# Decoder layer on one core: softmax sums divided out in token space, opening strips issued by three queues, and the shared expert's second layer of three batches moved behind the routed blocks

## The chip, the cores and the metric

The kernel runs on one core of a Trainium2 chip. The core has five engines that run their own instruction streams: PE (TensorE, matmuls and transposes, with its weight loads shown as PEld), DVE (VectorE), ACT (ScalarE), POOL (GpSimd) and SP (SyncE, which here only issues DMAs; POOL and ACT can issue them too). They meet by semaphores. The metric is the time of one execution in device microseconds. The profile is one execution, recorded by the hardware.

## The reference

`x` has 4 batches of 512 tokens with 256 channels. Three layers follow each other, each with a LayerNorm before it and added to `x`: two state-space blocks over the sequence, cross attention to `ctx` (16 heads of 16 channels), and a mixture of experts with a shared expert.

```
x = x + ssm_blocks(layernorm(x))
# attention, on ctx with 512 keys, 16 heads of 16
q = layernorm(x) @ Wq.T + bq;  k = ctx @ Wk.T + bk;  v = ctx @ Wv.T + bv
attn = softmax(q_h @ k_h.T / 4)            # per head, 512 x 512
x = x + concat_h(attn @ v_h) @ Wo.T + bo
# feed-forward
xt = layernorm(x)
probs = softmax(xt @ Wg); the two largest of 8 experts, their weights scaled to sum 1
moe = sum of the two: weight * gelu(xt @ Wu[e]) @ Wd[e]
x = x + moe + gelu(xt @ W1) @ W2           # the shared expert
```

The change touches how the softmax's sums are divided out, how q and k get to their place at the start of attention, and when `gelu(...) @ W2` runs.

## The kernel before, in words

Everything is float32; attention's scores use the same bits as FP32R. The three layers are three phases, with a barrier between them (`phase_border`).

**Attention.** A *unit* `u` is half the heads (eight) of one batch; `NU` = 8 units run one after the other. `project(b)` makes a batch's q and k in six steps on PE: two sets of transposes of the normalised tokens (`xn`), then `k`, `q`, `k`, `q` for 128 channels each; four `v` steps follow. ACT adds the bias and rounds to the high part (`part`, L1001), DVE makes the low part (L1044). `strips` then copies rows of 16 partitions of `part` into `qk`, by small SBUF-to-SBUF DMAs, so that each head's high and low parts stand in one strip of 64 rows. A batch has 64 such DMAs; SP issues 40 and POOL 24 (`n % 8 in (1, 4, 6)`). Batch 0 is copied in two halves, one per unit (32 KB each, semaphores `first_in` and `strips_in`), later batches whole (64 KB each), and only once the last score of the batch two before is done, since `qk` has two places.

Before a unit's scores, DVE must know the largest score of every query row: `pe_max` computes a score tile only for this (L927) and DVE reduces it (L1069). The maxima are transposed to rows (`rows`, L901) and subtracted inside the score matmul (L947). A unit is 16 *slots*. In slot `s`, PE computes score tile `s` (L943, L947), the maximum tile of four slots ahead, which may belong to the next unit (the one after it from slot 12), then one *side* step if `side[(u, s)]` names one, and in odd slots the product with the values (L961). ACT takes the exponential of the score tile (L1008). Score and maximum tiles share three PSUM places of two banks, in a ring (`pair`). Side steps share one single bank (`NONE = 1`): a side step waits until the engine named in `TAKER` has emptied the bank of the one before. The opening runs `project(0)`, the `v` steps of batch 0, the 16 maxima of unit 0 with `project(1)` between the last of them.

The products with the values come out as channels by tokens, four heads in one bank, 32 rows a head, of which row 16 is the softmax sum. ACT copies the bank to `oT` (L1015). A side step `norm` then multiplies with the constant `spread` on PE (L906), which repeats each head's sum over its 32 rows; DVE takes the reciprocal of all 128x512 (L1060), and POOL multiplies `oT` with it (L1172). There are 16 such groups: group 0 of a unit has its `norm` in slot 12, group 1 in slot 1 of the next unit. Group 1 of an odd unit is followed by the output projection of the batch (`out`, L911, slots 3 to 6 of even units), which waits for POOL.

The steps that the slots name: `v` of the next batch in slots 7 to 10 of even units, `project(b + 2)` in slots 3 to 8 of odd units, `rows` in slot 13. The LayerNorm statistics of the next phase and of the batch after next run on DVE and ACT in slots 12 to 15 of even units.

**Feed-forward.** PE makes the shared expert's hidden layer for four batches (L1290), with the routing on DVE beside it, then its second layer (`pe_outputs`, L1300, 32 matmuls a batch; DVE adds them to `xres`, L1530). Then 39 blocks of 128 routed rows run: POOL gathers the rows (L1551), PE transposes, multiplies (L1337), transposes, multiplies (L1352), DVE weighs, POOL scatters to `y_choice` in DRAM (L1557). When all scatters have landed SP loads the results back (L1584), DVE adds two results per token (L1546, `xres` by batch) and SP stores the batches (L1587).

## Time and profile before

| | |
|---|---|
| median of three runs | 1961.38 us (1948.68 to 1962.60) |
| profiled execution | 1958.21 us, its span 1956.6 us |
| busy over the span | PE 87%, DVE 62%, POOL 53%, ACT 43% |
| scan stage (state-space blocks) | 0 to about 1217 us |
| opening of attention | 1219 to 1295 us: PE busy 42.8 us, clock 0.70, DMA share 0.36 |
| units 0 to 7 and the last outputs | 1295 to 1687 us: PE busy 308.9 us, DVE 231.0, ACT 159.7, POOL 47.5, clock 0.87 |
| feed-forward up to the shared second layer | 1687 to 1743 us: PE busy 54.4 us, clock 0.83 |
| shared second layer | 1743 to 1772 us: PE busy 28.8 us, clock 1.00 |
| routed blocks | 1772 to 1932 us: PE busy 159.4 us, clock 1.00 |
| the end | 1932 to 1957 us: PE busy 0.5 us, DVE 10.3, DMA share 0.80 |

The clock is the one that PE was granted, as a share of 2.4 GHz; its two levels are 1.2 and 2.4 GHz. A wait is idle time of an engine, put down to the instruction that ended it; it costs time only if the waiting engine is itself waited for.

### The profile page before, as it was taken

The numbers are of one execution on the slowest core, as the hardware profiler recorded it, in microseconds if no ns is written. First come the engines' busy times: TensorE is split into PE (matmuls) and PEld (weight loads), VectorE is DVE, ScalarE is ACT, GpSimd is POOL, SyncE is SP. The second block draws the span as 40 slices with busy tenths as digits, with TensorE's granted clock in tenths as the row PEclk, the third lists the DMA queues.
The fourth block names the chain that finished last, engine by engine and source line by source line (L and its number), as shares of the span: only waits on it lengthen the run. The fifth ranks groups of instructions, "written<-read, shape, count | busy, mean of one in ns | idle before, by whom it ended". The sixth has DMA issues, their size and how long they took to land.

```text
span 1956.6 us, 27123 instructions
## 1 busy us (share of the span) xinstructions
PE 1705.7 (87%) x10954; PEld 1298.8 (66%) x10954; DVE 1209.4 (62%) x1345; ACT 846.5 (43%) x1188; POOL 1034.0 (53%) x832
## 2 busy tenths in 40 slices
PE   5579899999999999999999998576777889799995
PEld 2468778978978978978879987232332333667763
DVE  3575677777767777766767795465574675233333
ACT  4556546546546446546446442133343346211110
POOL 1557858958948948858859885420200200012441
PEclk9889999999999999999999998688887889799997
DMA  3000000100001001001001210350310400411124
GB/s 140 39 22 34 33 22 23 44 22 29 38 23 40 27 22 45 22 22 45 23 22 77 84 47 13 80 93 32 66 32 6 80 1 1 178 60 36 65 65 158
DMA packets 38123, 93.62 MB, mean 48 GB/s; under 512 B 9137, under 2 KB 21809, under 8 KB 33521
## 3 DMA queue, kind: packets, MB, share of 16 engines
q1 hardware_dynamic: 30416, 75.37, 12.0%
q0 software_dynamic: 7584, 16.53, 3.3%
q8 instruction: 88, 1.44, 0.3%
q14 instruction: 35, 0.28, 0.0%
HBM read 65.52 MB, written 9.57 MB: 38 GB/s over the span
## 4 chain that ended last, share of the span: by engine, by line
PE 63%; POOL 11%; DVE 11%; issue 8%; ACT 3%; SPq 3%; DMA 1%; DVEq 0%; POOLq 0%; ACTq 0%
PE psum L423 18%; POOL hst L688 8%; PE psum L406 7%; PE psum L362 5%; PE psum L1352 3%; PE psum L1337 3%; PE psum L961 3%; PE psum L397 2%; DVE hst L523 2%; DVE uw L448 2%; DVE w_early L1060 2%; PE psum L911 2%; PE psum L943 2%; PE psum L893 2%; POOL filt L666 2%
## 5 line engine op out<-in xcount | busy, mean ns | idle before, releaser
L688 POOL TENSOR_TENSOR hst<-hst,cb 128x512 f32<-128x512 f32 x512 | 662.4, 1314 | 276.6 <-DVE hst L523 275.4
L523 DVE TENSOR_TENSOR_SCAN hst<-dA,psum 128x512 f32<-128x512 f32 x512 | 616.7, 1215 | 294.0 <-PE psum L423 263.1
L423 PEld LDWEIGHTS psum<-filt,c_early 128*128 128x128 f32 x2560 | 316.5, 195 | 56.4 <-issue 29.1
L423 PEld LDWEIGHTS psum<-filt,uT 128*128 128x128 f32 x2560 | 313.7, 194 | 48.4 <-issue 23.4
L423 PE MATMUL psum<-filt,c_early 128*128 128x112 f32 (+1 forms) x2560 | 321.6, 274 | 19.1 <-DVE hst L523 9.5
L423 PE MATMUL psum<-filt,uT 128*128 128x112 f32 (+1 forms) x2560 | 318.9, 272 | 19.2 <-DVE hst L523 9.8
L406 PE MATMUL psum<-ident,hst 128*128 128x128 f32 x2048 | 315.6, 278 | 12.7 <-POOL hst L688 12.0
L406 PEld LDWEIGHTS psum<-ident,hst 128*128 128x128 f32 x2048 | 246.0, 156 | 16.4 <-POOL hst L688 16.0
L626 ACT ACTIVATE dA<-delta,alog 128x512 f32<-128x512 f32 x256 | 181.1, 720 | 133.6 <-DVE hst L523 133.6
L626 ACT ACTIVATE dA<-xres,alog 128x512 f32<-128x512 f32 x256 | 179.5, 719 | 108.0 <-DVE hst L523 107.9
L1008 ACT ACTIVATE pT<-psum 128x1024 f32<-128x1024 f32 x128 | 128.3, 1024 | 197.8 <-PE psum L947 197.2
L1069 DVE TENSOR_REDUCE nmax<-psum 128x2 f32<-128x1024 f32 x128 | 153.5, 1215 | 75.8 <-PE psum L927 75.7
L1172 POOL TENSOR_TENSOR oT<-oT,w_early 128x512 f32<-128x512 f32 x16 | 20.3, 1268 | 330.7 <-DVE w_early L1060 330.7
L362 PE MATMUL psum<-xnT,w_early 128*128 128x512 f32 x256 | 127.4, 627 | 3.1 <-DVE hst L523 1.9
L666 POOL TENSOR_TENSOR filt<-toep,bcol 128x2240 f32<-128x2240 f32 x32 | 129.2, 4038 | 0.0
L448 DVE SCALAR_TENSOR_TENSOR uw<-xraw,w_cv,uw 128x512 f32<-128x512 f32 x96 | 123.3, 1287 | 7.4 <-ACT uw L561 5.2
L1404 ACT ACTIVATE hb<-psum 128x512 f32<-128x512 f32 x39 | 23.3, 598 | 166.5 <-PE psum L1337 166.5
L927 PE MATMUL psum<-qk 64*128 64x512 f32 x256 | 63.2, 497 | 36.4 <-DMA qk<-part 18.0
L1557 POOL DMA_INDIRECT y_choice<-yb,goal x39 | 38.5, 987 | 100.6 <-DVE yb L1521 100.6
L943 PEld LDWEIGHTS psum<-qk 64*128 64x128 f32 x256 | 26.5, 204 | 89.7 <-issue 53.5
L961 PE MATMUL psum<-pT,vt 128*32 128x512 f32 x512 | 76.8, 682 | 7.4 <-ACT pT L1008 7.4
L1551 POOL DMA_INDIRECT xb<-x_hat,origin x39 | 37.9, 972 | 84.0 <-DVE gate_at L1505 72.4
(193 smaller groups left out, 2104.4 us busy)
## 6 DMA issues: line engine op xcount, KB each, us to landing
cb<-c_rows SPq DMA_DIRECT2D x32, 1024.0 KB, 4.7
qk<-part SPq DMA_DIRECT2D x120, 64.0 KB, 2.4
qk<-part POOLq DMA_DIRECT2D x72, 64.0 KB, 4.2
w_up<-up_dram SPq DMA_DIRECT2D x8, 512.0 KB, 7.5
w_down<-down_dram SPq DMA_DIRECT2D x8, 512.0 KB, 14.2
w_up<-y_choice SPq DMA_DIRECT2D x8, 512.0 KB, 8.2
qk<-part SPq DMA_DIRECT2D x80, 32.0 KB, 2.0
xm<-x_dram SPq DMA_DIRECT2D x4, 512.0 KB, 9.0
```

The costliest lines, as they stand in the source:

```text
L362: i = pe.matmul(bk, w_in[:, l, kt, m8 * P:(m8 + 1) * P], xnT[:, kt, :], start=kt == 0, stop=kt == KD - 1)
L406: m = pe.matmul(psum[:, Y0 + et, t * P:(t + 1) * P], hst[:, i % NH, t * P:(t + 1) * P], ident[:], start=n == 0 and t == 0, stop=n == NSTAT ...
L423: m = pe.matmul(bk[:, c * QC:c * QC + CH[c]], uT[k % 2][:, c, et * P:(et + 1) * P], filt[:, f % 2, c, n % GN, 0:CH[c]], start=True, stop=True)
L448: dve.scalar_tensor_tensor(out=dst, in0=xraw[:, j, tap:tap + S], scalar=w_cv[:, l, j, tap:tap + 1], in1=dst, op0=ALU.mult, op1=ALU.add).th ...
L523: dve.tensor_tensor_scan(hst[:, i % NH, :], dA[:, i % NDA, :], bank("v", i), 0.0, ALU.mult, ALU.add).then_inc(scan_done, 1)
L626: act.activation(dA[:, a % NDA, :], delta[k % 2][:, et, :], ACT.Exp, scale=alog[:, k // B, et, n:n + 1]).then_inc(decay_done, 1)
L666: pool.tensor_tensor(filt[:, f % 2], toep[:, :].unsqueeze(1).unsqueeze(1).to_broadcast([P, NCH, GN, QC]), bcol[:, k % 2, :, g * GN:(g + 1) ...
L688: pool.tensor_tensor(h, h, cb[:, q % 2, i // ET % GN, :], ALU.mult).then_inc(g_done, 1)
L943: pe.matmul(o[:, e, :], qk[k0:k0 + KR, b % 2, 1, j, half, kv * P:(kv + 1) * P], qk[k0:k0 + KR, b % 2, 0, j, half, :], start=True, stop=Fal ...
L961: m = pe.matmul(psum[i * HROW:(i + 1) * HROW, PV, :], vt[:, cp, kv, c0:c0 + HROW], pT[:, (m0 + i // 2) % NPT, i % 2, :], start=kv == 0, st ...
L1008: act.activation(pT[:, m % NPT], pair(u, "score", s), ACT.Exp, scale=HDIM ** -0.5).then_inc(pair_act, 1)
L1069: dve.tensor_reduce(nmax[:, u % 2, t, 2 * j:2 * j + 2], pair(u, "max", r), AX.X, ALU.max, negate=True).then_inc(pair_dve, 1)
```

## The change

Four things are changed.

1. *Sums in token space.* `spread`, the 128x512 reciprocal and POOL's product go. A group now takes two side steps. `sums`: PE transposes the four 128x128 tiles of `oT` to tokens by channels; DVE takes the reciprocal of the 16 sums of a row (`rc`) and multiplies the bank by it, each over its head's 32 columns, into `otok`. `norm`: PE transposes `otok` back and ACT copies the bank to `oT`. `out` waits for that copy. POOL has no work but its DMAs.
2. *Order.* `sums` stands in slots 1 and 12, `norm` in 2 and 14, `project(b + 2)` in 3, 4, 5, 7, 9, 11, `out` in 4, 5, 6, 8, `v` in 3, 7, 10, 15. POOL issues its strips of a batch as soon as they may go.
3. *Opening strips.* Batch 0's 64 DMAs a half are issued by SP (24), POOL (24) and ACT (16, ahead of its square root for the second LayerNorm). Later batches stay at 40 and 24.
4. *Shared second layer.* Only batch 0's stays ahead of the routed blocks. That of batches 1 to 3 comes behind the last block, in the four banks which the blocks have left, and DVE's additions of it stand between those of the routed results.

```diff
-            shrink = w_early[:, KD * 2 * P:KD * 2 * P + S]
+            rc = sb(ac, "rc", [P, TB, 4])
+            otok = w_early[:, KD * 2 * P:KD * 2 * P + S]
-            SP_STRIPS, POOL_STRIPS = 40 * 16, 24 * 16
+            OPENING, LATER = (0, 2, 1, 0, 1, 2, 1, 0), (0, 1, 0, 0, 1, 0, 1, 0)
+            FIRST = [16 * UH * OPENING.count(z) for z in range(3)]
+            STRIPS = [16 * UH * LATER.count(z) for z in range(2)]
...
                 if u:
-                    slot(u, 1, u - 1, "norm", 1)
+                    slot(u, 1, u - 1, "sums", 1)
+                    slot(u, 2, u - 1, "norm", 1)
                 if u % 2 == 0:
                     for t in range(TB):
                         if b:
-                            slot(u, 3 + t, b - 1, "out", t)
+                            slot(u, (4, 5, 6, 8)[t], b - 1, "out", t)
                         if b + 1 < B:
-                            slot(u, 7 + t, b + 1, "v", t)
+                            slot(u, (3, 7, 10, 15)[t], b + 1, "v", t)
                 elif b + 2 < B:
-                    for n, name in enumerate(project(b + 2)):
-                        slot(u, 3 + n, *name)
-                slot(u, 12, u, "norm", 0)
+                    for s, name in zip((3, 4, 5, 7, 9, 11), project(b + 2)):
+                        slot(u, s, *name)
+                slot(u, 12, u, "sums", 0)
                 if u + 1 < NU:
                     slot(u, 13, u + 1, "rows", 0)
+                slot(u, 14, u, "norm", 0)
...
+                elif what == "sums":
+                    pe.wait_ge(group_out, group(x, j) + 1)
+                    for t in range(TB):
+                        i = pe.transpose(bk[:, t * P:(t + 1) * P], oT[:, x % 2 * UG + j, t * P:(t + 1) * P], ident[:])
                 elif what == "norm":
-                    pe.wait_ge(group_out, group(x, j) + 1)
-                    i = pe.matmul(bk, spread[:], oT[:, x % 2 * UG + j, :], start=True, stop=True)
+                    pe.wait_ge(*taken(x, "sums", j))
+                    for t in range(TB):
+                        i = pe.transpose(bk[:, t * P:(t + 1) * P], otok[:, t * P:(t + 1) * P], ident[:])
                 elif what == "out":
                     if j == 0:
-                        pe.wait_ge(normed, group(2 * x + 2, 0))
+                        pe.wait_ge(*taken(2 * x + 1, "norm", UG - 1))
...
+                elif what == "norm":
+                    act.wait_ge(*filled_by_pe(x, "norm", j))
+                    act.copy(oT[:, x % 2 * UG + j, :], one(x, "norm", j)).then_inc(taken(x, "norm", j)[0], 1)
...
                     if x == (1, "xn", 0):
+                        strips(act, 2, 0)
                         act_ln_root(LN2[1], TB, 2 * TB)
...
-                elif what == "norm":
-                    dve.wait_ge(*filled_by_pe(x, "norm", j))
-                    dve.reciprocal(shrink, one(x, "norm", j)).then_inc(taken(x, "norm", j)[0], 1)
+                elif what == "sums":
+                    v = one(x, "sums", j).rearrange("p (t i r) -> p t i r", t=TB, r=HROW)
+                    dve.wait_ge(*filled_by_pe(x, "sums", j))
+                    dve.reciprocal(rc[:], v[:, :, :, HDIM]).then_inc(rc_done, 1)
+                    dve.wait_ge(rc_done, group(x, j) + 1)
+                    dve.tensor_tensor(otok.rearrange("p (t i r) -> p t i r", t=TB, r=HROW), v, rc[:].unsqueeze(3).to_broadcast([P, TB, 4, HROW]),
+                                      ALU.mult).then_inc(taken(x, "sums", j)[0], 1)
...
-            def pool_norm(u, g):
-                o = oT[:, u % 2 * UG + g, :]
-                pool.wait_ge(*taken(u, "norm", g))
-                pool.tensor_tensor(o, o, shrink, ALU.mult).then_inc(normed, 1)
...
-                for b in range(B):
+                for b in range(NEAR):
                     pe_outputs(b)
...
+                for b in range(NEAR, B):
+                    pe_outputs_late(b)
...
-                for b in range(B):
-                    r = xres[:, toks(b), :]
-                    dve.wait_ge(y_loaded[b], 16 * TOPK)
-                    for k in range(TOPK):
...
+                for b in range(NEAR, B):
+                    dve_outputs_late(b)
+                    dve_choices(b - 1)
+                dve_choices(B - 1)
```

How the change moves instructions is seen on three engines. First ACT in the opening of attention. Before, behind the four high parts of batch 0 (L1001):

```order
L989 COPY axnT<-psum 128x512 x2
L1001 ACTIVATE part<-psum,b_qk 128x512 x4
L115 ACT_TABLE_LOAD
L115 ACTIVATE stat<-stat,epst 128x4
L989 COPY axnT<-psum 128x512 x2
```

And now:

```order
L1000 COPY axnT<-psum 128x512 x2
L1014 ACTIVATE part<-psum,b_qk 128x512 x4
L1165 DMA qk<-part 16x512 x32
L115 ACT_TABLE_LOAD
L115 ACTIVATE stat<-stat,epst 128x4
L1000 COPY axnT<-psum 128x512 x2
```

Thirty-two DMA issues, sixteen for each half, came between the high parts and the square root (L115), for whose result DVE waits ahead of its first maximum.

Second PE in slots 3 to 6 of unit 3 (an odd unit; L884 or L889 are transposes of `xn`, L893 or L898 the projections). Before:

```order
L893 MATMUL psum<-c_early,w_early 128x512 x2
L961 MATMUL psum<-pT,vt 32x512 x4
L943 MATMUL psum<-qk 128x512 x2
L947 MATMUL psum<-nrow,pick 128x512 x2
L927 MATMUL psum<-qk 128x512 x2
L893 MATMUL psum<-axnT,w_early 128x512 x2
```

And now, from the same `k` step on:

```order
L898 MATMUL psum<-c_early,w_early 128x512 x2
L972 MATMUL psum<-pT,vt 32x512 x4
L954 MATMUL psum<-qk 128x512 x2
L958 MATMUL psum<-nrow,pick 128x512 x2
L938 MATMUL psum<-qk 128x512 x2
L954 MATMUL psum<-qk 128x512 x2
L958 MATMUL psum<-nrow,pick 128x512 x2
L938 MATMUL psum<-qk 128x512 x2
L898 MATMUL psum<-axnT,w_early 128x512 x2
```

Between the `k` and the `q` step there was one slot's score and maximum tile; now there are two slots' worth.

Third DVE behind the last routed block (L1521 or L1550 is the weighing of a block). Before:

```order
L1521 TENSOR_SCALAR yb<-psum,gate_at 128x256
L1513 COPY ht<-psum 128x512
L1521 TENSOR_SCALAR yb<-psum,gate_at 128x256 x2
L1546 TENSOR_TENSOR xres<-xres,w_up 128x1024 x8
```

And now:

```order
L1550 TENSOR_SCALAR yb<-psum,gate_at 128x256 x2
L1565 TENSOR_TENSOR xres<-xres,psum 128x512 x2
L1559 TENSOR_TENSOR xres<-xres,w_up 128x1024 x2
L1565 TENSOR_TENSOR xres<-xres,psum 128x512 x2
L1559 TENSOR_TENSOR xres<-xres,w_up 128x1024 x2
L1565 TENSOR_TENSOR xres<-xres,psum 128x512 x2
L1559 TENSOR_TENSOR xres<-xres,w_up 128x1024 x4
```

The additions of the shared outputs of batches 1, 2 and 3 (L1565) now stand each ahead of the routed results of the batch before (L1559).

## Rows read from the trace of the kernel before

**Rows 1.** Timeline of attention's opening: start us, us, engine line op out<-in [idle before <-releaser].

```profile
1225.70 25.29 SPq L1144 DMA_DIRECT2D qk<-part  x40
1228.34 1.28 ACT L115 ACT_TABLE_LOAD   x1
1237.51 1.42 DVE L124 TENSOR_SCALAR xm<-xres,stat 128x256 f32<-128x256 f32 x4
1251.03 25.24 SPq L1147 DMA_DIRECT2D qk<-part  x40
1253.27 11.40 DVE L1069 TENSOR_REDUCE nmax<-psum 128x2 f32<-128x1024 f32 x10 [14.00 <-PE psum L927]
1265.36 3.78 PE L893 MATMUL psum<-c_early,w_early 128*128 128x512 f32 x4
1269.71 1.98 PE L893 MATMUL psum<-axnT,w_early 128*128 128x512 f32 x4
1277.77 1.27 ACT L1001 ACTIVATE part<-psum,b_qk 128x512 fp32r<-128x512 f32 x2 [12.45 <-DMA qk<-part]
```

**Rows 2.** Windows: stretch, length, busy us of PE, PEld, DVE, ACT, POOL, PEclk, DMA share, GB/s.

```profile
1226.00:1238.00 12.00, 8.46 (x20) 3.42 (x18) 6.63 (x17) 2.88 (x4) 12.00 (x25) 1.00 0.52 109
1252.00:1276.00 24.00, 16.43 (x40) 6.75 (x40) 12.62 (x11) 1.17 (x2) 0.00 (x0) 0.63 0.24 52
```

**Rows 3.** Waits of PE, 1295 to 1665 us: us in total, times, longest.

```profile
PE psum L901 <- DVE w_early L1060: 22.5, 7, 4.3
PE psum L893 <- DVE part L1044: 13.5, 6, 2.3
PE psum L911 <- POOL oT L1172: 8.0, 3, 2.7
PE psum L884 <- ACT axnT L989: 2.7, 2, 1.4
```

**Rows 4.** The windows view, unit 3.

```profile
1455.00:1512.00 57.00, 41.04 (x170) 15.60 (x166) 27.06 (x24) 18.03 (x22) 2.54 (x2) 0.80 0.00 0
```

**Rows 5.** Timeline, PE: a projection of unit 3, row transposes of unit 5.

```profile
1468.28 3.78 PE L893 MATMUL psum<-c_early,w_early 128*128 128x512 f32 x4 [1.36 <-ACT axnT L989]
...
1596.12 0.66 PE L901 MATMUL psum<-ident,nsplit 128*128 128x128 f32 x4 [2.63 <-DVE w_early L1060]
```

**Rows 6.** Timeline of unit 4's first slots, and of the last output projections.

```profile
1515.13 0.59 ACT L1015 COPY oT<-psum 128x512 f32<-128x512 f32 x1 [1.55 <-PE psum L961]
1518.52 3.35 DVE L1060 RECIPROCAL w_early<-psum 128x512 f32<-128x512 f32 x1
1523.36 3.75 PE L911 MATMUL psum<-w_early,oT 128*128 128x256 f32 x8 [2.67 <-POOL oT L1172]
1529.81 1.99 PE L911 MATMUL psum<-w_early,oT 128*128 128x256 f32 x8
...
1673.37 10.00 PE L911 MATMUL psum<-w_early,oT 128*128 128x256 f32 x32 [4.88 <-POOL oT L1172]
```

**Rows 7.** Timeline, the shared expert's second layer on PE, and one addition.

```profile
1743.57 20.93 PE L1300 MATMUL psum<-raw,hs_own 128*128 128x256 f32 x96
1764.34 7.07 PE L1300 MATMUL psum<-raw,xm 128*128 128x256 f32 x32
1764.54 0.69 DVE L1530 TENSOR_TENSOR xres<-xres,psum 128x512 f32<-128x512 f32 x1 [2.76 <-PE psum L1300]
```

**Rows 8.** Timeline of the end.

```profile
1928.87 3.62 PE L1352 MATMUL psum<-w_down,ht 128*128 x16
1935.84 7.74 SPq L1584 DMA_DIRECT2D w_up<-y_choice  x8
1951.10 2.48 DVE L1546 TENSOR_TENSOR xres<-xres,w_up 128x1024 f32<-128x1024 f32 x2 [0.45 <-DMA w_up<-y_choice]
```

**Rows 9.** Timeline: SP's strips of batch 3, and their first use by PE.

```profile
1512.38 34.40 SPq L1153 DMA_DIRECT2D qk<-part  x40
1556.02 0.40 PE L927 MATMUL psum<-qk 64*128 64x512 f32 x2
```

114 lines of the change are left out of this document (65 added, 49 removed).

## The prediction

> **What bounds the kernel now.** The profiled execution took 1958.2 us (span 1956.6), between the runs' extremes and 3 us under their median of 1961.4; the sum below is against 1958.2, and I take the median as moving by the same amount. First I read the page's 40 slices. The scan stage, up to about 1217 us, runs the same instructions in both kernels, so I leave it. Then the timeline of the opening of attention, the waits of TensorE in attention's eight half-batches ("units"), and the timeline of the last 30 us.
>
> - Opening [rows 1]. Nothing can start before the query and key strips are copied. The 40 copies of the first half take SP 25.3 us, so 0.632 each, and the first row maximum starts 2.3 us after the last issue. The second half goes out at the same pace, and ScalarE, which must not overwrite `part`, stands until 1277.8. DMA engines are 52% busy with two queues issuing and 24% with SP alone [rows 2]: issuing is the limit, not moving.
> - Units [rows 3]. TensorE is the nearest to full, but it waits in a few places: 22.5 us in seven waits behind the 3.35 us reciprocal, 13.5 us in six waits for a projection's bank, 8.0 us in three waits for GpSimd's product, 2.7 us in two waits behind ScalarE's copies (the transposes of xm; the projection after them waits the same way). Where it waits, its clock falls: 0.80 in unit 3 [rows 4], and a projection of four matmul records takes 3.78 us there [rows 5] against 1.98 at 2.4 GHz [rows 1].
> - End [rows 7, 8]. Shared outputs of one batch take 7 us of TensorE at full clock, then 39 routed blocks run on a full TensorE. After its last matmul (1932.5) the span goes on for 24.1 us with TensorE empty: the scatters land, results are loaded back, and VectorE adds four times 2.48 us.
>
> **The shared outputs moved behind the blocks.** Three batches take from 1743.6 to 1764.3, 20.8 us [rows 7]. TensorE ends where it did, at 1932.5, but the last block leaves it 20.8 us earlier. SP's loads then start at 1915.0 instead of 1935.8, and the last batch of results, which VectorE took up at 1951.1, is there by 1930.3 [rows 8]. So the scatters and loads are hidden. Late outputs of batch 3 end at 1932.5; VectorE adds them (0.7), then batches 2 and 3 of the choices (2 x 2.48): 1938.4. The last add ended at 1953.6 and the span 3.0 us later [rows 8]; the new end is 1941.4. **-15.2**. The first block's gather loses 20.8 us of cover; the one batch of outputs that stays gives it 6.9, and it is issued about when that batch starts. I cost it at nothing; without the cover it would be some 3 us, once.
>
> **Opening on three queues.** SP issues 24 per half, GpSimd 24 as before, ScalarE 16. First half ready at 1225.7 + 24 x 0.632 + 2.3 = 1243.2, second at 1225.7 + 48 x 0.632 + 2.3 = 1258. But ScalarE's 32 issues stand ahead of its table load and square root for the second LayerNorm, and VectorE needs that root before its first maximum. No row shows a DMA issued by ScalarE; I take SP's 0.632. ScalarE is free at 1228.3, so the issues end at 1248.5; table load 1.28, then root, reciprocal, scaling (1.42) and a cast, which I estimate at 2.6 us together: first maximum at 1252.4, as against 1253.3. So the first half gives 0.9 us only. The second half gives more: the projection was there at 1265.4 + 3.8 = 1269.1, its ScalarE step ran at 1277.8, and now can at 1268.2: 9.6 us, the 0.9 included. The next projection, hidden in that stall, comes out of it: 2. **-7.6.** Bounds: if an issue cost half of 0.632 the maxima would start at the strips' 1243, 9 us more; if SP and ScalarE take turns, at 1.26 each, see the second rival: +8.
>
> **Sums in token space.** Per group of four heads, sixteen times: out go one 128x512 matmul, the reciprocal (3.35) and GpSimd's product; in come two times four transposes (0.66 the four [rows 5]), a reciprocal of 16 columns, a 128x512 product out of PSUM (0.69, as the addition of [rows 7]) and a ScalarE copy of 0.6 [rows 6]. The small reciprocal lies between nothing and 0.25; with it VectorE holds the bank for 1.0 instead of 3.35.
> - Seven waits at slot 13: 7 x 2.35 = -16.5.
> - GpSimd's product is off the path: three waits, -8.0; but what follows the norm now finds the bank until ScalarE's copy behind an exponential, 1.36 as in [rows 3], in slot 3 of three units: +4.1. The same in slot 15, where a value projection now stands (three units): +4.1.
> - Norm of group 1 in slot 2 waits for VectorE about 0.4, eight times: +3.
> - TensorE: two sets of transposes (1.2) for about 1.05: +0.2 sixteen times, +3.
> - Unit 7 has no maxima and is paced by ScalarE's exponentials; two copies more: +1.2.
> - After the last values the chain reciprocal, product was 4.9 us of idle TensorE [rows 6]; now 1.0 + 0.7 + 0.6 + gaps = 2.5: -2.4.
> - Clock: the first output projection after the GpSimd wait took 3.75, others 1.99 [rows 6]: three times 1.7; and about 1 after each of three slot-13 waits in odd units: -8.
>
> Together **-19.5**. GpSimd loses its work; it had no waiter but these.
>
> **Projections at slots 3, 4, 5, 7, 9, 11.** One slot between them does not empty the single side bank in time: bank free 2.5 us after the next score, and a slot's own TensorE work is about 1.2. So 2.25 becomes 1.3: six times, -5.7. The two waits behind ScalarE (1.36) stay. Six of the eight projections run wholly or partly at 1.2 GHz, up to 1.9 us over 1.98; 11 us with the value matmuls between. With less idle I give back about 7. **-12.7.** The later start of SP's batch strips costs nothing: they wait for the unit's last score anyway. Their cover gets thin, though: issued over 34.4 us from 1512.4, landed near 1549, needed at slot 12 at 1556 [rows 9]. The 12 slots before lose about 5 us here, which leaves 2.
>
> Sum: -15.2 - 7.6 - 19.5 - 12.7 = -55.0, so 1958.2 - 55 = **1903 us**.
>
> The Trainium skill ("DMA: Bandwidth & Descriptors", Rules for kernel authors) says that spreading DMAs over SP, ACT and GpSimd does not help bandwidth and only saves issue time. By that rule, with issue time small, the opening would give nothing and the sum be 1911. [Rows 2] speak against it here: with engines half idle, issue time is what SP spends.
>
> **The rivals.**
> - *Descriptors made in turn.* If SP's and ScalarE's issues exclude each other, both cost 1.26: ScalarE ends at 1228.3 + 40.4 = 1268.7, VectorE starts its maxima at 1272.5, 19 us later than before, and gets back the 9.6 us stall: +8 instead of -7.6, **1919 us**. For it: nobody but SP has been seen on that kind of queue. Against it: GpSimd's issues beside SP's change SP's pace by nothing (25.29 with them, 25.24 mostly without [rows 1]), though they are of another kind. The skill's "Perfetto Trace Analysis", DMA Instruction — HWDGE, has the descriptor generator locked for exclusive use by one sequencer; by it this rival holds. 15 in 100.
> - *Waits move instead of going.* If the clock gives nothing back and strips or LayerNorm hold slots 12 to 15, half of 32 us is left: **1919 us** too; with the first rival 1935. 20 in 100.
> - *The clock comes back everywhere.* Less idle puts all of attention near 2.4 GHz and the waits overlap: another 20 us, **1883 us**. 15 in 100.
> - *The side bank becomes the bound, slower than before.* There are 15 norms and 15 sums in the units, and each with its successor passes one bank. If every one costs TensorE 2.25 as projections do, and 2 more at half clock, that is 30 x 4.25 = 127 less the 12 counted; minus the 55: **2018 us**. It decides from about 2.2 us for each. Against it: sums leave through VectorE in 1.0, and the step behind is a whole slot later. 3 in 100.
>
> The forecast (1892 to 1914) has 47 in 100. Range: down to the clock case, 1880, and up to 1932, short of both bad cases together. Within 1% (about what a measurement of this kernel can tell from no change) means above 1939 here: 3 in 100; slower by over 1%, 3 in 100.
>
> **What would show it.** Last matmul near 1878 (1932.5 less the 40 of attention), then under 10 us to the end. ScalarE: 32 issues of 0.63 ending some 20 us after they start, the first maximum barely earlier, and no stall of 8 us at the eleventh. Waits before the row transposes under 1 us. Unit 3 shorter by about 10 us at a clock nearer 0.9. Wrong if ScalarE's issues take 1.2, if TensorE waits over 2 us before each norm or side projection, or if maxima of the batch after next wait for strips.

## The result, and the profile of the changed kernel

The changed kernel takes **1883.59 us** (median of 4 runs, 1882.49 to 1885.21) beside 1961.99 for the kernel before on the same chip: ratio 0.9621, 95% interval 0.9585 to 0.9656. The forecast was 1903 with a range of 1880 to 1932. The direction and the range hold; the forecast was 19 us too high.

The profiled execution took 1885.21 us (span 1883.6) as against 1958.2 (1956.6): 73.0 us less. The medians moved by 78.4, because the profiled execution before lies 4 us below its median; the forecast was 55 against the profiled one, so the account below is of 73.0, and 18 us are missing. Read from the two timelines, stage by stage, in us:

| stage | before | after | difference | forecast |
|---|---|---|---|---|
| scan, to attention's first transposes | 1217.95 | 1219.34 | +1.4 | 0 |
| opening, to unit 0's first exponential | 78.2 | 66.0 | -12.2 | -7.6 |
| units, to the last group's copy | 370.5 | 325.9 | -44.6 | -29.8 |
| tail, to the feed-forward's first transpose | 21.1 | 17.1 | -4.0 | -2.4 |
| feed-forward's opening, to the first shared outputs | 55.8 | 57.4 | +1.6 | 0 |
| shared outputs and blocks | 188.9 | 189.3 | +0.4 | 0 |
| behind TensorE's last matmul | 24.1 | 8.5 | -15.6 | -15.2 |

**Opening.** The timeline of the changed kernel, as in [rows 1] (start, length, engine, what, in brackets the idle time before it and who ended it):

```profile
1227.09 30.98 SPq L1165 DMA_DIRECT2D qk<-part  x48
1227.38 23.10 POOL L1165 DMA_DIRECT2D qk<-part  x48 [7.51 <-DVE part L1064]
1229.03 21.07 ACTq L1165 DMA_DIRECT2D qk<-part  x32
1250.18 1.28 ACT L115 ACT_TABLE_LOAD   x1 [20.47 <-issue]
1253.66 11.39 DVE L1091 TENSOR_REDUCE nmax<-psum 128x2 f32<-128x1024 f32 x10
1265.75 3.05 PE L898 MATMUL psum<-c_early,w_early 128*128 128x512 f32 x4
1268.92 0.69 ACT L1014 ACTIVATE part<-psum,b_qk 128x512 fp32r<-128x512 f32 x1 [3.20 <-PE psum L898]
1269.16 1.98 PE L898 MATMUL psum<-axnT,w_early 128*128 128x512 f32 x4
```

ScalarE issues 32 strips in 21.07 us, 0.658 each, while SP issues 48 in 30.98, 0.645 each; SP alone took 0.632 [rows 1]. So the two do not take turns. The table load stands behind ScalarE's issues at 1250.2, as the forecast had it, and the first maximum comes at 1253.7. ScalarE writes `part` at 1268.9 where it had stood until 1277.8: the stall is gone.

**Units.** Waits of TensorE in the changed kernel, 1281 to 1650 us (in total, times, longest), as in [rows 3]; L906 are the row transposes, L914 the `norm` step:

```profile
PE psum L902 <- ACT oT L1018: 13.2, 5, 4.7
PE psum L938 <- ACT pT L1025: 8.4, 20, 0.4
PE psum L906 <- DVE w_early L1081: 7.8, 5, 2.4
PE psum L914 <- DVE w_early L1081: 6.6, 8, 1.2
PE psum L898 <- DVE part L1064: 5.2, 6, 0.9
PE psum L910 <- DVE part L1064: 4.5, 2, 2.2
```

Slot 13's wait (L906) fell from 22.5 to 7.8, the projections' from 13.5 to 5.2, GpSimd's 8.0 are gone. Of what the projections lost, 4.5 have only moved: their last step is now in slot 11, and the `sums` of slot 12 (L910) wait for its bank. New is a wait of 13.2 before value projections (L902), behind ScalarE's norm copy: 4.7, 4.4 and 1.4 in slot 15 of units 0, 2 and 4, the rest in slot 3. Gone is a wait of the kernel before that the forecast did not name:

```profile
PE psum L961 <- ACT pT L1008: 6.9, 2, 3.5
```

TensorE waited there in units 0 and 2 for an exponential, because ScalarE does its layer norm's root between two exponentials. ScalarE is as late as before, but in the changed kernel the value projection of slot 15 stands ahead of that product and takes the wait. Now the whole of units 0 to 6, in the windows view (stretch, length, TensorE's busy us, granted clock, DMA share, GB/s), before and after:

```profile
1296.00:1648.00 352.00, 278.81 (x1365) 0.87 0.21 40
```
```profile
1285.00:1591.00 306.00, 252.54 (x1440) 0.96 0.24 46
```

TensorE is idle 53.5 us instead of 73.2: -19.7. It is busy 252.5 us instead of 278.8: -26.3, with more records (entries of the profiler for a matmul), not fewer. Of the 46 us a good half is not waiting that went, but the same kinds of instruction running faster, at a clock of 0.96 instead of 0.87. By unit the clock was 0.89, 0.84, 0.90, 0.81, 0.87, 0.90, 0.88 before (units 0 to 6) and is now 0.89, 0.96, 0.91, 0.96, 1.00, 1.00, 1.00. The projections of unit 3 (1430 to 1478), as in [rows 5], groups by line (busy us, mean ns of one | idle before):

```profile
L898 PE MATMUL psum<-c_early,w_early 128*128 128x512 f32 x8 | 4.0, 619 | 2.2 <-ACT axnT L1000 1.4 <-DVE part L1064 0.9
L898 PE MATMUL psum<-axnT,w_early 128*128 128x512 f32 x8 | 4.0, 618 | 1.7 <-DVE part L1064 1.7
```

The sixteen records take 0.62 us on average (0.59 to 0.70); before, the two groups of that unit took 1.04 and 1.01.

**End.** As in [rows 8]:

```profile
1854.18 13.98 PE L1301 MATMUL psum<-raw,hs_own 128*128 128x256 f32 x64
1857.69 8.12 SPq L1625 DMA_DIRECT2D w_up<-y_choice  x8
1867.99 7.07 PE L1301 MATMUL psum<-raw,xm 128*128 128x256 f32 x32
1875.10 0.69 DVE L1565 TENSOR_TENSOR xres<-xres,psum 128x512 f32<-128x512 f32 x1 [2.77 <-PE psum L1301]
1875.71 4.87 DVE L1559 TENSOR_TENSOR xres<-xres,w_up 128x1024 f32<-128x1024 f32 x4
```

SP's loads of the results run under 21 us of shared outputs; behind TensorE only 0.69 and 4.87 us of additions and the store are left.

### The profile page after: what moved, and what is told of

It reads as the page before. It is cut to its first block, busy times and chain, and to the rows that moved or that the text cites. A ratio compares the mean times of both kernels' runs of the same rounds, so it can differ in the third digit from the quotient of the medians.

```text
span 1883.6 us, 27335 instructions
## 1 busy us (share of the span) xinstructions
PE 1680.0 (89%) x11050; PEld 1295.4 (69%) x11050; DVE 1170.0 (62%) x1361; ACT 854.4 (45%) x1204; POOL 1012.8 (54%) x816
## 3 DMA queue, kind: packets, MB, share of 16 engines
q1 hardware_dynamic: 29248, 74.25, 12.5%
## 4 chain that ended last, share of the span: by engine, by line
PE 66%; POOL 11%; DVE 10%; issue 7%; ACT 4%; ACTq 1%; DMA 0%; DVEq 0%; SPq 0%; POOLq 0%
PE psum L423 18%; POOL hst L688 8%; PE psum L406 7%; PE psum L362 5%; PE psum L1379 3%; PE psum L1364 3%; PE psum L972 3%; PE psum L397 3%; DVE hst L523 2%; DVE uw L448 2%; PE psum L954 2%; DVE nmax L1091 2%; PE psum L898 2%; POOL filt L666 2%; PE psum L919 2%
## 5 line engine op out<-in xcount | busy, mean ns | idle before, releaser
L406 PE MATMUL psum<-ident,hst 128*128 128x128 f32 x2048 | 316.0, 278 | 12.7 <-POOL hst L688 11.9
L1176 POOL DMA_DIRECT2D qk<-part x72 | 34.3, 485 | 202.6 <-PE psum L938 175.4
L1433 ACT ACTIVATE hb<-psum 128x512 f32<-128x512 f32 x39 | 23.3, 598 | 146.1 <-PE psum L1364 146.1
L938 PE MATMUL psum<-qk 64*128 64x512 f32 x256 | 59.4, 465 | 28.0 <-DMA qk<-part 10.7
L362 PEld LDWEIGHTS psum<-xnT,w_early 128*128 128x128 f32 x256 | 48.6, 204 | 44.2 <-issue 39.5
L1364 PE MATMUL psum<-w_up,xt 128*128 x156 | 73.4, 593 | 0.8 <-DVE xt L1538 0.8
```

The lines of the kernel that those rows point to most:

```text
L362: i = pe.matmul(bk, w_in[:, l, kt, m8 * P:(m8 + 1) * P], xnT[:, kt, :], start=kt == 0, stop=kt == KD - 1)
L406: m = pe.matmul(psum[:, Y0 + et, t * P:(t + 1) * P], hst[:, i % NH, t * P:(t + 1) * P], ident[:], start=n == 0 and t == 0, stop=n == NSTAT ...
L938: m = pe.matmul(o[:, e, :], qk[k0:k0 + KR, b % 2, 0, j, half, t * P:(t + 1) * P], qk[k0:k0 + KR, b % 2, 1, j, half, :], start=True, stop=T ...
L1364: m = pe.matmul(psum[:, U0 + j % 2, :], xt[:, j % NXT, kt, :], w_up[:, bass.ds(at + kt * F, F)], start=kt == 0, stop=kt == KD - 1)
```

## The experiments

Theory 1: the waits went about as forecast, and what the forecast lacks is TensorE's clock, which comes back once its waits are short. Theory 2, the rival: the clock belongs to the stretch, and the missing time lies in waits or transfers that the forecast priced wrongly. Three things were read of each: the median, the span's stages, and TensorE's idle and busy time in windows of units.

**The changed kernel once more**, beside the next three.

> The changed kernel itself, once more beside the three that follow, so that they can be compared on the same chip. Both theories: 0.960 to 0.962 of the kernel before, 1883 to 1888 us.

1884.84 us (1879.59 to 1887.42), ratio 0.9603 (0.9587 to 0.9619), span 1883.2. Its units and opening are within 0.2 us of the first profile; opening 66.2, first to last exponential 323.6. "Against the changed kernel" below means this span.

**Useless work in the waits of the kernel before.**

```
-                            pe_max(*maxima_at(u, s))
+                            pe_max(*maxima_at(u, s), times=5 if u in (1, 3) and 4 <= s <= 9 else 1)
```

> The kernel before the change, with the matmul pair of each maximum tile written five times over in slots 4 to 9 of units 1 and 3 (the same values into the same place: eight matmuls more a slot, 96 in all, that nothing needs). They fall where TensorE now waits for the side bank for about a microsecond and more a slot, so they turn idle time into busy time and add no other work. Theory 1 (the granted clock falls because of the waits): the clock of unit 3's window (0.81 before) rises to 0.88 or more and unit 1's (0.84 to 0.89) with it, the useful matmuls there run shorter, and the time stays within 5 us of the kernel before or falls, although some 0.2 us times 96 = 20 us at full clock of PE work is added, of which the waits hide 8 to 12. Theory 2 (clock independent of waits): the clock stays at 0.81 and the time rises by the added work less the idle time it fills, +8 to +16.

1952.54 us (1950.88 to 1953.19), ratio 0.9948 (0.9934 to 0.9961): more work and 10 us less time. Units 1, 2 and 3 in the windows view, before and with the extra work:

```profile
1340.00:1398.00 58.00, 41.97 (x192) 0.84 0.02 3
1398.00:1455.00 57.00, 45.51 (x224) 0.90 0.44 81
1455.00:1516.00 61.00, 44.62 (x196) 0.81 0.03 5
```
```profile
1344.00:1398.00 54.00, 42.06 (x244) 0.96 0.03 5
1398.00:1455.00 57.00, 45.88 (x216) 0.88 0.43 79
1455.00:1510.00 55.00, 43.25 (x248) 0.94 0.03 6
```

The clock of the two filled units rises from 0.84 and 0.81 to 0.96 and 0.94, that of unit 2 between them, not filled, does not. They get 4.2 and 6.6 us shorter. Unit 3's groups show how, before and filled (the maxima's matmuls, then the projections):

```profile
L927 PE MATMUL psum<-qk 64*128 64x512 f32 x34 | 7.8, 454 | 0.8 <-ACT pT L1008 0.8
L893 PE MATMUL psum<-c_early,w_early 128*128 128x512 f32 x8 | 7.1, 1036 | 3.6 <-DVE part L1044 2.3 <-ACT axnT L989 1.4
L893 PE MATMUL psum<-axnT,w_early 128*128 128x512 f32 x8 | 6.8, 1006 | 4.5 <-DVE part L1044 4.5
```
```profile
L928 PE MATMUL psum<-qk 64*128 64x512 f32 x82 | 13.4, 416 | 0.8 <-ACT pT L1009 0.8
L893 PE MATMUL psum<-c_early,w_early 128*128 128x512 f32 x8 | 4.0, 619 | 1.8 <-DVE part L1045 1.3 <-ACT axnT L990 0.4
L893 PE MATMUL psum<-axnT,w_early 128*128 128x512 f32 x8 | 4.0, 618 | 2.7 <-DVE part L1045 2.7
```

The added records cost 5.6 us, the projections lose 5.9 of busy time and 3.6 of waiting. Theory 2 wanted +8 to +16 at an unchanged clock; it falls here. In these units TensorE's clock fell because of its waits. The filling does not take them all: unit 3 is still idle for 11.7 us instead of 16.4. Nor does the sum of idle time order the clocks: in the changed kernel unit 1 is idle 11.5 us of 47.8 at 0.96, its longest wait 2.2 us, and unit 0 only 7.0 of 43.5 at 0.89, but one of its waits lasts 4.7.

**Projections close together again.**

```
-                    for s, name in zip((3, 4, 5, 7, 9, 11), project(b + 2)):
+                    for s, name in zip((3, 4, 5, 6, 7, 8), project(b + 2)):
```

> The changed kernel, with the projections of batch b+2 in slots 3 to 8 (one a slot, as before the change) instead of 3, 4, 5, 7, 9, 11. The forecast's own size for this part: idle +5.7 us over two odd units and +7 us of clock, so about +12.7 over the changed kernel (1896). Theory 1 (the waits went as forecast, and the rest of the gain is the granted clock of TensorE coming back once they are short): the windows of units 1 and 3 (1329 to 1376 and 1430 to 1478 us, both at 0.96 now) fall to 0.90 or below, TensorE is busy some 7 to 10 us longer there and idle 6 longer, +13 to +17 (1897 to 1901). Theory 2 (the clock has nothing to do with the order of the side work, it is the stretch's own): clock of these windows stays within 0.02 of 0.96, the time moves by the idle time alone, +5 to +6 (1889).

1902.18 us (1890.69 to 1904.78), ratio 0.9680 (0.9654 to 0.9706); span 1900.5, +17.3. Units 1 and 3:

```profile
1329.00:1385.00 56.00, 41.52 (x206) 0.85 0.02 3
1441.00:1495.00 54.00, 39.30 (x206) 0.91 0.04 4
```

Unit 1 is 8.4 us longer at a clock of 0.85, unit 3 6.4 longer at 0.91; both had 0.96. From first to last exponential the idle time is 5.9 us more, as forecast (5.7), and the busy time 11.9 (7 forecast), with the same instructions. Theory 1 holds, by a little more than it gave (+13 to +17); the forecast's clock term was too small.

**The old division back** (spread matmul, reciprocal of 128x512, product on GpSimd, which issues its strips behind its products).

```
-                    slot(u, 1, u - 1, "sums", 1)
-                    slot(u, 2, u - 1, "norm", 1)
+                    slot(u, 1, u - 1, "norm", 1)
...
-                slot(u, 12, u, "sums", 0)
+                slot(u, 12, u, "norm", 0)
-                slot(u, 14, u, "norm", 0)
...
+                    dve.reciprocal(shrink, one(x, "norm", j)).then_inc(taken(x, "norm", j)[0], 1)
```

> The changed kernel with the old way of dividing the sums out: matmul against the spread matrix (slot 12 and slot 1), 128x512 reciprocal on VectorE, product on GpSimd, GpSimd's strips behind its products; opening, projections' slots and end as changed. The forecast's own size for this part is 19.5 us, of which 8 are clock: 1903. Theory 1 (the forecast's idle times are right, and the clock gives more than it was given): idle of TensorE over units 0 to 6 comes back by 11 to 13 us and its busy time by 12 to 20, together +24 to +33 (1908 to 1917), and the odd units, which have both the projections and the reciprocals, lose more than the even ones. Theory 2 (some of the gain lies in another part than the forecast had it, in transfers that GpSimd now issues earlier): the loss shows in the first maxima of a batch waiting for strips, not in slots 12 and 13, and the clock of the windows moves by under 0.02; +12 or less.

1901.79 us (1899.21 to 1904.93), ratio 0.9693 (0.9680 to 0.9706); span 1898.1, +14.9. Both theories missed: less than theory 1's 24, and clocks that move by up to 0.10, which theory 2 excludes. Idle time is +5.5 in the units and +3.4 in the tail, busy time +5.5 in the units (334.6 us with 275.0 busy, against 323.6 with 269.5). The waits and the units tell why. Slot 13's waits are back at 21.1 us, but the 13.3 before the value projections are gone. Units 3, 5 and 6 are 3.8, 5.2 and 4.8 us longer (the last two at 0.90 and 0.91 instead of 1.00), but units 0 and 2 are 2.5 and 3.4 *shorter*: in them the new order has a value projection in slot 15 behind the norm copy of slot 14. So the new division costs something in even units, which is tried below. Now the two parts side by side, from first to last exponential: 368.3 us before, 341.3 with the new division and close projections, 334.6 with the old division and spread projections, 323.6 with both. Taken out of the changed kernel one at a time the parts are worth 17.7 and 11.0 us of the 44.8 by which the two kernels differ. Most of the other 16 is a third part that neither run put back, the output projections one slot later. With the old division and the new slots GpSimd's product still comes before them, but TensorE no longer waits for it:

```profile
1386.74 1.99 PE L914 MATMUL psum<-w_early,oT 128*128 128x256 f32 x8
```

Before, this first output projection of a batch came behind a wait of 2.67 us and took 3.62, 3.75 and 3.50 in the three units. So 8.0 of idle time and 4.9 of clock are the later slot's, not the division's, to which the forecast gave them. The three parts come to 41.6: they add but for 3 us. (No run moves that slot alone.)

**Opening without ScalarE's queue.**

```
-            OPENING, LATER = (0, 2, 1, 0, 1, 2, 1, 0), (0, 1, 0, 0, 1, 0, 1, 0)
+            OPENING, LATER = (0, 1, 0, 0, 1, 0, 1, 0), (0, 1, 0, 0, 1, 0, 1, 0)
...
-                        strips(act, 2, 0)
```

> The changed kernel with the opening strips on SyncE's and GpSimd's queues alone (40 and 24 a batch, as later batches have them), none issued by ScalarE; the waits for the first and the second half stay apart. Forecast's size for the opening: 7.6 us for both changes to it, of which the ScalarE issues were to cost as much at the first maximum as they win (-0.9) and to win the 9.6 us stall at the second half. Theory 1 (both halves' transfers end by the number of issues on the longest queue, 0.645 us each): SyncE's second half ends 8 issues a half later, 16 x 0.645 = 10.3 us, the stall before the second half's maxima is back with 3 to 8 us, while the first maximum comes 2 us sooner or later than 1253.7; +4 to +12 over the changed kernel (1888 to 1896). Theory 2 (the gain is from the split of the semaphore into two halves, not from the third queue): 0 to +2 (1884 to 1886).

1893.67 us (1892.4 to 1895.27), ratio 0.9651 (0.9636 to 0.9666); span 1891.9. From attention's start to the first exponential 78.3 us, +12.2, all that the opening had gained, so splitting the semaphore in two halves gives nothing by itself. (The span shows only +8.7, because the feed-forward's opening ran 5.5 us shorter, see below.) The stall in its timeline:

```profile
1280.26 1.27 ACT L1014 ACTIVATE part<-psum,b_qk 128x512 fp32r<-128x512 f32 x2 [12.37 <-DMA qk<-part]
1282.92 3.59 PE L898 MATMUL psum<-c_early,w_early 128*128 128x512 f32 x4 [0.34 <-DVE nmax L1090]
```

ScalarE waits for SP's strips, and the projection behind the stall takes 3.59 us where the same one (the second k of `project(1)`) took 1.98 in the changed kernel, and the row transposes behind it 1.08 instead of 0.63. That is the part of the opening's gain that the forecast lacks: the stall (10 us, counted from attention's start) takes some 2 us of clock with it. And the q projection that was to cost 2 costs nothing: it is done while ScalarE and VectorE round the k before it, and in both kernels the next k projection starts 2.66 us after ScalarE's write. Theory 1 holds.

**The root between ScalarE's two halves of issues.**

```
-                        strips(act, 2, 0)
+                        first_strips(act, 2, 0, first_in[2])
                         act_ln_root(LN2[1], TB, 2 * TB)
+                        first_strips(act, 2, 1, second_in[2])
```

> The changed kernel with one step moved on ScalarE: it issues the first half's 16 opening strips, then does the layer norm's root (table load and one activation), then issues the second half's 16, instead of 32 issues and then the root. Theory 1 (the first maximum waits for the root, as VectorE's program has the layer norm ahead of the maxima, and the root stands behind 32 issues of 0.658 us): the root runs at about 1240 instead of 1251.5, VectorE's first maximum comes as the first half's strips do, at about 1247 instead of 1253.66; the maxima end 6 us sooner and the second half's ScalarE strips, 1.6 us later, are still in time: -6.4 (-4 to -7). Theory 2 (the end of the opening is set by the second half's strips or by the work on TensorE after them, so the early maxima only wait later): a stall of 4 us or more appears before the second half's first maxima (k of the second half), and the time falls by under 2 us.

1878.68 us (1875.12 to 1880.0), ratio 0.9574 (0.9561 to 0.9587); span 1875.2.

```profile
1240.32 1.28 ACT L115 ACT_TABLE_LOAD   x1 [10.39 <-issue]
1248.08 11.40 DVE L1092 TENSOR_REDUCE nmax<-psum 128x2 f32<-128x1024 f32 x10 [4.20 <-PE psum L938]
```

VectorE now waits for the strips, not for the root; the first maximum comes 7.8 us earlier and the first exponential 6.7 (59.4 instead of 66.1, both from attention's start; expected 6.4). No stall follows: ScalarE's longest wait for a projection is 3.5 us. Theory 1 holds. (The median falls by 6.2; the span's -8.0 has 3.9 of the feed-forward's opening in it, see below.)

**Value projections out of slot 15.**

```
-                            slot(u, (3, 7, 10, 15)[t], b + 1, "v", t)
+                            slot(u, (3, 7, 9, 10)[t], b + 1, "v", t)
```

> The changed kernel with the four values' products of the next batch in slots 3, 7, 9, 10 instead of 3, 7, 10, 15 of the even units: none behind slot 14's norm transposes, whose copy ScalarE makes late (behind the exponentials, and in two units behind the layer norm's table loads). TensorE waited 4.4 to 4.7 us in each of three units before the value product of slot 15, and the product behind it took 3.65 to 3.78 us, twice its time at full clock. Theory 1 (wait and half clock both belong to that place): -(1.4 to 4.7) a unit of wait, three units, and 1.9 a unit of clock, -8 to -14. Theory 2 (ScalarE is late by then whatever stands in the side bank, and the next slot's score product waits in its place): the wait moves to L938 or L958 on the scores' bank, 0 to -3.

1877.45 us (1873.07 to 1877.96), ratio 0.9563 (0.9550 to 0.9576); span 1875.8. Of TensorE's waits two rows changed by more than 0.5 us:

```profile
PE psum L972 <- ACT pT L1025: 6.5, 2, 3.2
PE psum L902 <- ACT oT L1018: 2.7, 2, 1.4
```

L902 falls from 13.3 to 2.7, but 6.5 us come up at L972, the products with the values, which need ScalarE's exponential: in two units ScalarE is late by its layer norm's table loads, whoever waits for it, as at L961 in the kernel before. (The text above counts 4.4 to 4.7 us in each of three units; it was so in two, 1.4 in the third.) Units 0, 2 and 4 are 2.8, 2.4 and 0.7 shorter, unit 1 is 1.9 longer: -4.0 over the units, half of what theory 1 wanted, more than theory 2 gave. The feed-forward's opening gave 5.6 more to this run's span, and attention started 2.5 later.

**All shared outputs ahead of the blocks again** (`NEAR = 4`, VectorE's choices in one row at the end).

> The changed kernel with the shared expert's second layer for all four batches ahead of the routed blocks, as before the change. Theory 1 (these matmuls last the same on either side of the blocks, and behind them they cover the gather and addition of the last choices): TensorE ends at the same time (within 1 us), the span ends 24 us behind it instead of 8.5: +15 (+13 to +16). Theory 2 (the transfers that the end waits for start later by TensorE's clock or the first block waits for its gathered rows): less than +10, and a wait of the first block for the gather is not there or TensorE ends sooner.

1898.54 us (1896.76 to 1900.91), ratio 0.9682 (0.9668 to 0.9695). TensorE ends at 1871.82 and the span 23.3 us behind it, as against 8.5: **+14.8**. TensorE's end was to stay within 1 us and is 2.9 sooner; here too the feed-forward's opening was the shorter one (3.9 us), which has nothing to do with the end. In its timeline the results are loaded when TensorE has nothing left:

```profile
1875.17 6.97 SPq L1623 DMA_DIRECT2D w_up<-y_choice  x8
1880.61 2.49 DVE L1559 TENSOR_TENSOR xres<-xres,w_up 128x1024 f32<-128x1024 f32 x2 [8.27 <-DMA w_up<-y_choice]
```

Theory 1 holds for what lies behind TensorE's end. Shared outputs and blocks last 188.8 us in this order and 189.0 in the other.

**VectorE's order at the end.**

```
-                dve_choices(B - 1)
+                dve_choices(B - 2)
+                dve_choices(B - 1, ahead=True)
+                dve_outputs_late(B - 1)
```

(`ahead` leaves out the wait for the shared outputs' additions; the last additions then wait for the choices, and SP's last stores for them.)

> The changed kernel with the end of VectorE's program in another order: the choices of batches 2 and 3 before the last batch's two additions of the shared expert's outputs, so that VectorE adds them as TensorE finishes instead of waiting for them with 8.6 us of choices left to do; SyncE's last store waits for them. Now the span ends 8.5 us after TensorE's last matmul, of which VectorE has 2 x 2.77 of waiting earlier on and 4.87 of choices behind it. Theory 1 (VectorE's order sets the end): end 4.3 us sooner (-3 to -5), the last store following the second addition at once. Theory 2 (the last choice's rows, gathered by GpSimd, or the store set it): VectorE waits for y_choice instead, 0 to -1.

1882.91 us (1881.0 to 1883.71), ratio 0.9595 (0.9582 to 0.9608), which the medians do not tell from the changed kernel's. The end does:

```profile
1868.44 7.07 PE L1301 MATMUL psum<-raw,xm 128*128 128x256 f32 x32
1874.27 2.48 DVE L1560 TENSOR_TENSOR xres<-xres,w_up 128x1024 f32<-128x1024 f32 x2 [0.15 <-DMA w_up<-y_choice]
1877.21 1.29 DVE L1568 TENSOR_TENSOR xres<-xres,psum 128x512 f32<-128x512 f32 x2 [0.46 <-DVE xres L1560]
```

6.0 us behind TensorE instead of 8.5, so 2.5 less and not 4.3, between the two theories: the last choice's rows are loaded only at 1874.3, so both additions of the shared outputs still come after TensorE's end (1875.5).

**The three edits together.**

> The changed kernel with the three edits together: the root between ScalarE's two halves of opening strips, the values' products in slots 3, 7, 9, 10, and VectorE's new order at the end. Alone they gave -6.6 from attention's start to its first exponential, -4.0 over the units, and -2.5 behind TensorE's last matmul; the rest of what two of them gained in the span (3 to 6 us) was the clock of the feed-forward stage's opening, 57.9 instead of 63.5 us from attention's outputs to the sends, which two other runs (one of them with a longer opening) had as well. Theory 1 (edits add, and the feed-forward's opening has its clock by something that no edit here touches): 1883 - 13 = 1870 with the slow opening of that stage, 1865 with the other. Theory 2 (the edits take time from the same waits): 1873 to 1876.

**1868.55 us** (1866.06 to 1869.19), ratio 0.9523 (0.9510 to 0.9536): 16 us under the changed kernel and the best here. Span 1866.2: opening 59.4 (-6.7), units 319.4 (-4.2), end 5.8 (-2.7); they add, as theory 1 had it. The feed-forward's opening gives 5.6 more, and attention starts 2.3 later: the span's -17.0.

**Ten matmuls more while TensorE waits for the feed-forward's layer norm**, on top of the three edits.

```
+            def pe_fill(times):
+                for _ in range(times):
+                    pe.matmul(psum[:, PV, :], ident[:], w_v[:, 0, :], start=True, stop=True)
...
+                pe_fill(10)
```

> The kernel with the three edits, and ten 128x128x512 matmuls more behind attention's last output, into the sums' free bank, that nothing reads: TensorE does them while it would wait 4.38 us for VectorE's layer norm ahead of the feed-forward stage (10 x 0.43 = 4.3 us at full clock). Theory 1 (the granted clock falls behind a wait of that length; keep TensorE busy and it does not): transposes, gates and hidden layers of that stage run at or near full clock, 57.9 or less from outputs to sends instead of 57.9 to 63.5, so -2 to -7 against the kernel without the ten. Theory 2 (the low clock there comes from the work itself, 64 gate matmuls of 8 columns, which take 9.5 to 12.5 us): gates as before, 0, or +1 if the ten outlast the wait.

1873.73 us (1872.36 to 1874.37), ratio 0.9551 (0.9537 to 0.9564): 5 us *slower*. One cause is my price: such a matmul is two records, so the ten take 8.75 us, not 4.3, and outlast the wait of 4.38 by 4.4. The other is in the rows, without them and with them:

```profile
1618.10 5.38 PE L1389 MATMUL psum<-ident,xm 128*128 128x128 f32 x32 [4.38 <-DVEq L96]
1624.40 9.98 PE L1338 MATMUL psum<-w_g,xn 128*128 128x8 f32 x64 [0.92 <-ACT xn L1422]
```
```profile
1611.81 8.75 PE L980 MATMUL psum<-w_early,ident 128*128 128x512 f32 x20
1620.79 3.69 PE L1398 MATMUL psum<-ident,xm 128*128 128x128 f32 x32 [0.24 <-PEq L96]
1625.67 12.65 PE L1347 MATMUL psum<-w_g,xn 128*128 128x8 f32 x64 [1.19 <-ACT xn L1431]
```

The transposes keep 2.4 GHz, 3.69 us instead of 5.38; the 64 gate matmuls behind them take 12.65, as in the changed kernel, at a granted clock of 0.60 in their first half and 0.50 in the second. Theory 1 holds for the transposes and falls for the gates. Whether the ten matmuls brought the gates from 9.98 to 12.65 is not shown: the same gates take either time in kernels without them (below).

**Fillers in the opening too** (22 ahead of the first maximum, 8 ahead of the row transposes).

> As the run before, and 22 such matmuls more in the opening while TensorE waits 10.7 us for the first strips, and 8 while it waits 3.6 us for the maxima's split: 40 in all, 17 us of TensorE's time at full clock, none of it needed. Theory 1 (clock falls behind waits): granted clock between 1238 and 1290 rises from 0.5 in most of it; the maxima there are VectorE's (1.13 us each), so only batch 1's projections (2.9 to 1.9 us) and the first score slots gain: -2 to -5 more than the run before. Theory 2: the fills only delay what stands behind them: 0 to +3.

1886.1 us (1879.94 to 1888.02), ratio 0.9608 (0.9594 to 0.9622), 17.6 slower than without fillers and 12.4 slower than with the ten: worse than either theory gave, as the price was wrong by half here too. The opening is 11.7 us longer, and the feed-forward's opening as long as with the ten. The 22 take 19.05 us where the wait was 10.7, the 8 take 7.13 where it was 3.6, and the clock does not stay: from the fifth maximum on, each pair of matmuls waits 0.34 us and more for VectorE's reduction and is back at half clock:

```profile
1238.04 19.05 PE L980 MATMUL psum<-w_early,ident 128*128 128x512 f32 x44
1258.84 0.50 PE L938 MATMUL psum<-qk 64*128 64x512 f32 x2 [0.86 <-DVE nmax L1101]
1262.24 0.79 PE L938 MATMUL psum<-qk 64*128 64x512 f32 x2 [0.34 <-DVE nmax L1101]
```

A short filler of the right length was not run.

## Why the prediction was right in sign and 19 us too high

- **Shared outputs behind the blocks, -15.2.** Right: -15.6 in the profile, -14.8 by the experiment that undoes it. Shared outputs and blocks last as long in either order, the first block's gather cost 0.3 us.
- **Opening, -7.6.** The mechanism is right: ScalarE's root behind its issues (first maximum 1253.3 before, 1253.7 after, which is 1.0 earlier counted from attention's start; forecast 0.9), the stall gone. Measured -12.2: the 2 us for the q projection were not paid, and 2 more came as clock behind the missing stall. The first rival, issues in turn, is refuted by 0.658 and 0.645 side by side. (Its +8 was a slip besides: 19 later and 9.6 back is +9.4.) The forecast had this rival hold by the Trainium skill's "Perfetto Trace Analysis", DMA Instruction — HWDGE. That went too far: the section gives one sequencer exclusive use of the descriptor generator until its descriptors are made, but no duration. What the trace excludes is exclusive use through most of an issue: two streams at 0.65 us leave each at most about 0.33, an estimate from these two rates. The other rule (the Trainium skill's "DMA: Bandwidth & Descriptors", Rules for kernel authors: another queue saves issue time only) agrees with the trace, but issue time and what hung on it were worth 12.2 us here.
- **Idle time in the units.** The forecast's terms without clock (-16.5, -8.0, +4.1, +4.1, +3 and -5.7) come to -19.0; measured -19.7. That they agree is luck in part, as errors cancel: slot 13's waits kept 7.8 instead of 6.0, slot 2's norms cost 6.6 instead of 3, slot 15 cost 10.5 instead of 4.1, and the projections' waits, with the 4.5 that moved to slot 12, kept 9.7 instead of 7.8. On the other side are waits that no term named: 6.9 before the products with the values (L961) and some 6 before the scores (L943, 6.6 before, 0.7 now).
- **The clock in the units: the step that failed.** "With less idle I give back about 7", and -8 for the division: 15 together. TensorE's busy time fell by 26.3 although, by the forecast's estimate, some 3 us of work were added: 29. That is 14 us more, and it is what the units gave beyond their forecast (44.6 instead of 29.8). The opening gave 4.6 more, tail and end 2.0; scan, feed-forward's opening and blocks took 3.4 of it back: the missing 18. I had priced the half clock only at the few instructions named (three output projections, three slot-13 waits, 11 us of projections), but the windows showed 0.81 to 0.90 in all of units 0 to 6. The rival "clock comes back everywhere" (another 20, 1883 us) had 15 in 100 and is the nearest to what happened: units 4 to 6 run at 1.00. But units 0 and 2 stay at 0.89 and 0.91 and the opening at 0.74 (0.70 before), so that its 1883 meets the median within a microsecond is luck. Unit 3, to be 10 shorter at nearer 0.9, is 13.3 shorter at 0.96. The filled kernel shows the cause, waits. By parts the clock gave 11.9 at the projections (7 forecast); 5.5 and the 3 of added work, 8.5, at the division without the output projections (3 forecast); and 4.9 at the output projections, as forecast (5.1), though by their later slot and not by the division. Some 3 us stay without an owner.
- **Signs.** The last matmul came at 1875.1, near the 1878 that the forecast named. But 1932.5 less 40 is 1892.5: the 1878 was a slip, and TensorE ended 17 us sooner than the sum meant. Waits before the row transposes were to be under 1 us; the longest is 2.4.
- **What nearly hid it.** The stretch from the first of attention's last output projections (L919) to the last matmuls ahead of the shared outputs (L1349) lasts 62.9 to 64.5 us in five profiles of four kernels here (the changed one twice, close projections, old division, VectorE's order) and 57.9 to 59.6 in those of five others, with the same instructions there (gates 12.6 us or 9.6 to 10.2); in the kernel before it is 63.1, gates 12.5. No edit touches it, and it moves spans by 4 to 6 us: differences of that size were read in stages. It need not belong to a kernel: one execution with close projections took 1890.69 us beside four of 1898.86 to 1904.78, but has no profile.

Open: what sets the clock in that opening. More TensorE work ahead of it did not raise it in the gates. While the gates run the DMA engines are full, in the short profiles as in the long ones (share 1.02 at 412 to 414 GB/s in the gates' second half, clock 0.50); no run moved those transfers.

## What to carry to other kernels

Where TensorE waits often, look at the granted clock by windows, and price a removed wait twice: once as idle, once as the time that the instructions around it lose to half clock over the whole stretch. Follow each wait to the instruction that has it afterwards, too, and ask of each which edit removes it (here GpSimd's waits went by one slot's delay, not by the product that was dropped): 4.5 us of the projections' waits and the one behind ScalarE's layer norm only changed place. A cheap test is to write useless matmuls into the waits: if the time falls, the clock is what you pay for. And on a queue's engine, ask what stands behind a row of DMA issues; half of them after the one short instruction that another engine needs gave 6.7 us here.

## What the runs showed of the hardware

- 96 matmuls that nothing needs made a kernel 10 us faster (1952.54 against 1962.63): clock 0.81 to 0.94 in the same unit.
- ScalarE and SP issue DMAs side by side at 0.658 and 0.645 us each; SP alone took 0.632.
- A stretch in which TensorE's records leave no gap can still be at half clock: the 64 gate matmuls of 8 columns took 12.65 us, at a granted clock of 0.60 and then 0.50, right behind transposes at 1.00.
- The same stage had two lengths, about 5 us apart, in profiles of kernels whose instructions there are the same; the cause is open.
